# A decoder layer on one core: where sixteen small products for the denominators are issued within a projection

## The chip, the cores and the metric

One core of one Trainium2 chip runs the whole kernel as one program. The metric is the device time of one execution in microseconds. Engines are TensorE (PE; its weight loads are listed apart as PEld), VectorE (DVE), ScalarE (ACT), GpSimd (POOL) and SyncE (SP, here the queue that issues most DMAs).

## What is computed

A post-norm decoder layer on x and a context, both (16, 512, 512), f32. Cut to the part around the change:

```python
qkv = x @ Wqkv.T                                   # 16 heads of 32
q, k = elu(q) + 1, elu(k) + 1
running_kv   = decay_scan(k * v)                   # out[t] = decay * out[t-1] + in[t]
running_ksum = decay_scan(k)
den = clip(sum(q * running_ksum, over a head's 32 channels), 1e-6)
out = q * running_kv / den
g = sigmoid(out @ Wgate.T + bgate)
out = (g * out + (1 - g) * v) @ Wout.T
x = layernorm(x + out)
x = layernorm(x + x * scan_0.9(ctx * ctx))
x = layernorm(x + ffn(x))                          # 4-bit weights, 16-bit activations, SiLU gate
```

## The kernel before

There are three phases: weights are split and quantised, then the attention phase, then the feed-forward phase. The attention phase takes the 16 batch entries one after the other in a pipeline of steps. Step s has a *front* half for batch entry s (q, k and v projections, scans, denominators, the quotient) and a *back* half for entry s - 1 (gate, output projection, the two layer norms). Step 0 has only a front, step 16 only a back, and steps 1 to 15 have both. Each engine has its program written out by hand in its own block, and semaphores join them; an engine executes its list in order.

Full products are made at about f32 precision from three fp32r matmuls of a high and a low half each (`product`, L761: high x high at L767, high x low at L768, low x high at L771), four times over the 512 contraction rows (k = 0 to 3). So one tile of a projection is twelve matmuls of 512 columns. `product` takes a function `between`, which it calls in each of the four rounds k, after the second matmul and ahead of the third.

The *denominators* are 16 products in each step: for each of four row groups j and each of four channel groups c, `qks[:, c]` (q times the running sum of keys, 128 x 128) is the stationary side and `head_sum[:, c]` (128 x 16, which adds up the channels of a head) the moving one, in plain f32 (L820). They land in `den_bank`, a part of the PSUM bank `qk_ps0`. The first call, j = 0, waits for `qks_ready`, that VectorE's last product L553 of the step has been written; the last matmul of j = 3 raises `den_ready`. In the trace each of these products is two instructions of 16 columns, 32 in a step; below they are called the narrow matmuls.

TensorE's order in a step with both halves is: q, k, v of the first channel tile (`qkv(s, 0)`), the gate's four tiles, `qkv(s, 1)`, the context carry, `qkv(s, 2)`, `qkv(s, 3)`, then the output projection in four tiles (`project`), whose results go alternately to two banks `mix_ps`. Between rounds of its second tile stand the denominators; inside its fourth, at k = 1, stands the turn of their reciprocals (L828), and behind it the broadcast of these over the channels (L836).

Who waits for what around that: VectorE adds each projection tile to the residual (`first_residual`, L590). Its order there is L553 `qks`, the residual of tile 0, the last scan and product of the front, two splits of the next x (L534), three local sums (L598), the residual of tile 1, then `reciprocals` (L631 to L637), which waits for `den_ready`. TensorE's turn (L828) waits for `recl_ready`, the last of these. Tiles 2 and 3 of the projection wait for the residual of the tile two before them. In step 0, which has no projection, the 16 products are issued one behind the other.

Of the kernel before, what the change touches and what calls it, by code (L numbers as in the profile page):

```python
# [20 lines left out]
TT = T // P  # L21
# [208 lines left out]
def attention_phase(nc, xT, x, ctx_in, b_gate, decay_in, wah, wal, x2_dram, amax_x2):  # L230
# [3 lines left out]
    with ExitStack() as ctx:  # L234
# [89 lines left out]
        with nc.Block() as block:  # L324
# [432 lines left out]
            def _(pe):  # L757
# [3 lines left out]
                def product(out, stat, mov, between=None):  # L761


                    n = len(stat)
                    for k in range(n):
                        (sh, sl_), (mh, ml) = stat[k], mov[k]
                        pe.matmul(out, sh, mh, start=(k == 0), stop=False)  # L767
                        pe.matmul(out, sh, ml, start=False, stop=False)  # L768
                        if between:
                            between(k)  # L770
                        mm = pe.matmul(out, sl_, mh, start=False, stop=(k == n - 1))  # L771
                    return mm
# [8 lines left out]
                def qkv(b, c):  # L781
                    n = KC * b + c
                    if c == 0:
                        pe.wait_ge(xl_ready, KC * (b + 1))


                    wait(pe, phi_ready, n - 1)
                    product(qk_ps[c % 2][:, 0], w_tile(0, c), x_halves)
                    product(qk_ps[c % 2][:, 1], w_tile(1, c), x_halves).then_inc(qk_ready, 1)
                    wait(pe, v_copied, n - 1)  # L790
                    if c == 0:
                        wait(pe, o_ready, KC * b)
                    product(v_ps[c % 2][:], w_tile(2, c), x_halves).then_inc(v_ready, 1)

                def gate(s):
                    pe.wait_ge(ol_ready, KC * s)
                    for m in range(KC):
                        if m >= 2:
                            pe.wait_ge(gated, KC * (s - 1) + m - 1)
                        product(mix_ps[(m + 1) % 2][:], w_tile(3, m), a_halves).then_inc(gate_ready, 1)  # L800

                def project(s, tiles, between=None):
                    if 0 in tiles:
                        pe.wait_ge(ml_ready, KC * s)
                    for j in tiles:
                        if j == 0:
                            pe.wait_ge(gated, KC * (s - 1) + 3)
                        elif j == 1:
                            pe.wait_ge(scanned, TT * s)
                        else:  # L810
                            pe.wait_ge(y_ready[0], TT * (s - 1) + j - 1)
                        stat = [tuple(h[:, k].rearrange("p (q j) -> p j q", j=TT)[:, j] for h in (ah, al)) for k in range(KC)]
                        mov = [(wah[:, k, 4], wal[:, k, 4]) for k in range(KC)]
                        product(mix_ps[(j + 1) % 2][:], stat, mov, between).then_inc(proj_ready, 1)

                def denominators(s, j):
                    if j == 0:
                        pe.wait_ge(qks_ready, KC * (s + 1))
                    for c in range(KC):
                        mm = pe.matmul(den_bank[:, j], qks[:, c, j * P:(j + 1) * P], head_sum[:, c],  # L820
                                       start=(c == 0), stop=(c == KC - 1))
                    if j == TT - 1:
                        mm.then_inc(den_ready, 1)

                def turn_reciprocals(s):
                    pe.wait_ge(recl_ready, s + 1)
                    for j in range(TT):
                        mm = pe.matmul(turn_bank[:, j * P:(j + 1) * P], rec_halves[:, j], ident_r[:], start=True, stop=True)  # L828
                    mm.then_inc(turned_ready, 1)

                def broadcast(s):

                    pe.wait_ge(rec_turned_ready, s + 1)
                    pe.wait_ge(v_copied, KC * (s + 1))
                    for c in range(KC):
                        pe.matmul(bc_banks[c], head_bc[:, c], rec_turned[:], start=True, stop=True).then_inc(bc_ready, 1)  # L836

                def context_carry(s):
                    pe.wait_ge(sql_ready, s)
                    pe.wait_ge(gated, KC * s)  # L840
                    product(carry_bank, [(strip_h[:], strip_l[:])], [(csq_h[:], csq_l[:])]).then_inc(carry_ready, 1)

                def step(s, front, back):
                    if front:
                        qkv(s, 0)
                    if back:
                        gate(s)
                    if front:
                        qkv(s, 1)
                    if back:  # L850
                        context_carry(s)
                    if front:
                        qkv(s, 2)
                        qkv(s, 3)
                    if back:
                        project(s, (0,))
                    if front and back:
                        project(s, (1,), lambda j: denominators(s, j))
                        project(s, (2,))
                        project(s, (3,), lambda k: turn_reciprocals(s) if k == 1 else None)  # L860
                    elif back:
                        project(s, (1, 2, 3))
                    else:
                        for j in range(TT):
                            denominators(s, j)
                        turn_reciprocals(s)
                    if front:
                        broadcast(s)

                step(0, True, False)  # L870
                with pe.Fori(0, (NB - 2) // 2) as i:
                    for u in range(2):
                        step(2 * i + 1 + u, True, True)
                step(NB - 1, True, True)
                step(NB, False, True)

# [998 lines left out]
```

## Time and profile before

| | us |
|---|---|
| median of 3 runs | 2744.77 (2744.38 to 2745.86) |
| the profiled execution | 2746.06 |
| its span, first to last instruction | 2744.3 |
| TensorE matmuls busy in the span | 2592.1 (94%) |
| TensorE weight loads | 2173.3 (79%) |
| VectorE | 1986.0 (72%) |
| ScalarE | 1362.9 (50%) |
| GpSimd | 404.6 (15%) |
| attention phase in the span | about 60 to 1090 |
| mean granted clock of TensorE | 0.973 |

The profile is of one execution, taken by the hardware profiler. Matmuls are pipelined: a matmul is listed with some 0.39 us, but the next one starts 0.23 us behind it, so the distance between starts is what one costs. The granted clock is given as a share: 1.00 is the upper level of TensorE's clock (2.4 GHz), 0.50 the lower (1.2 GHz). A view of stretches has these columns: the stretch, its length, busy time (and instructions started) of PE, PEld, DVE, ACT and POOL, then the granted clock, the DMA engines' busy share and GB/s. A row of a timeline gives start, length, engine, line, operation and tiles, the count of merged instructions, and in brackets the idle time before with what ended it.

### The profile page before, as it was taken

What the parts mean: (1) busy time and instruction counts of PE and PEld (TensorE: products, weight loads), DVE (VectorE), ACT (ScalarE), POOL (GpSimd) and SP (SyncE); (2) the same over time, 40 slices, a digit from 0 to 9 for tenths busy, and PEclk for the clock granted to TensorE, in tenths of its full rate; (3) what the DMA queues carried; (4) which work ended last, traced back from release to release, by engine and by line L of the source; (5) the groups of instructions that cost most, each with busy time, mean ns of one, the idle gap of its engine ahead of it and who ended that gap; (6) DMA issues with size and microseconds to landing.
All of it is one profiled execution on the core that took longest, in us unless ns stands there. A gap on an engine that the chain in (4) does not pass through costs nothing.

```text
span 2744.3 us, 32949 instructions
## 1 busy us (share of the span) xinstructions
PE 2592.1 (94%) x11584; PEld 2173.3 (79%) x11584; DVE 1986.0 (72%) x2689; ACT 1362.9 (50%) x1716; POOL 404.6 (15%) x277
## 2 busy tenths in 40 slices
PE   2999999999999995799999999999999889999998
PEld 1788888888888884588888887888888668888886
DVE  6688888888888885355555556987777776666664
ACT  2355555555555544333333336988888712222222
POOL 2000000000000000000000002322222143333332
PEclk7899999999999997899999999999999989999999
DMA  5102111111122111655555447776677554455552
GB/s 206 47 26 98 61 61 69 61 61 61 67 90 80 61 54 46 207 193 188 188 188 183 168 155 268 282 271 252 254 260 258 213 223 199 199 208 206 217 220 104
DMA packets 146960, 429.24 MB, mean 156 GB/s; under 512 B 74848, under 2 KB 83296, under 8 KB 106592
## 3 DMA queue, kind: packets, MB, share of 16 engines
q1 hardware_dynamic: 144176, 408.72, 40.9%
q10 hardware_dynamic: 2736, 19.92, 1.8%
q8 instruction: 25, 0.41, 0.1%
q14 instruction: 23, 0.19, 0.0%
HBM read 234.62 MB, written 177.21 MB: 150 GB/s over the span
## 4 chain that ended last, share of the span: by engine, by line
PE 55%; DMA 2%; issue 1%; DVE 1%; ACT 1%; POOL 0%; SPq 0%; POOLq 0%; DVEq 0%; ACTq 0%
PE ff_ps L1759 12%; PE ff_ps L1761 12%; PE ff_ps L1760 12%; PE ff_ps L1811 6%; PE ff_ps L1813 6%; PE ff_ps L1812 6%; DMA ff_raw<-x_rows 0%; PE ff_ps L1769 0%; DMA ff_gs<-gate_ints 0%; DMA ff_q<-x_ints 0%; DMA ff_raw<-gate_products 0%; DMA up_products<-ff_group 0%; ACT ff_up_abs L1285 0%; DVE ff_lo L1703 0%; DMA gate_products<-ff_group 0%
## 5 line engine op out<-in xcount | busy, mean ns | idle before, releaser
L1759 PE MATMUL ff_ps<-ff_hi,ff_wh 128*128 128x512 f32 x1536 | 601.4, 392 | 43.7 <-DVE ff_lo L1473 40.3
L1760 PE MATMUL ff_ps<-ff_lo,ff_wh 128*128 128x512 f32 x1536 | 599.7, 390 | 0.0
L1761 PE MATMUL ff_ps<-ff_hi,ff_wl 128*128 128x512 f32 x1536 | 599.6, 390 | 0.0
L1296 ACT ACTIVATE ff_group<-ff_ps,ff_scales 128x512 f32<-128x512 f32 x384 | 258.2, 687 | 317.2 <-PE ff_ps L1761 305.8
L1759 PEld LDWEIGHTS ff_ps<-ff_hi,ff_wh 128*128 128x128 f32 x1536 | 289.7, 189 | 104.3 <-DVE ff_lo L1473 40.6
L1761 PEld LDWEIGHTS ff_ps<-ff_hi,ff_wl 128*128 128x128 f32 x1536 | 289.7, 189 | 60.4
L1760 PEld LDWEIGHTS ff_ps<-ff_lo,ff_wh 128*128 128x128 f32 x1536 | 289.9, 189 | 59.9
L1811 PE MATMUL ff_ps<-ff_wh,ff_hi 128*128 128x512 f32 x768 | 299.6, 390 | 25.1 <-DVE ff_lo L1697 23.7
L1812 PE MATMUL ff_ps<-ff_wl,ff_hi 128*128 128x512 f32 x768 | 299.2, 390 | 0.0
L1813 PE MATMUL ff_ps<-ff_wh,ff_lo 128*128 128x512 f32 x768 | 299.2, 390 | 0.0
L1487 DVE TENSOR_REDUCE ff_gate_max<-ff_group 128x2048 f32 (+1 forms) x48 | 109.7, 2286 | 208.3 <-ACT ff_group L1296 208.3
L1447 ACT ACTIVATE ff_hi<-ff_sr 128x2048 fp32r<-128x2048 int16 x47 | 90.2, 1920 | 337.8 <-PE ff_ps L1813 325.9
L767 PE MATMUL qk_ps<-xh,wah 128*128 128x512 f32 x512 | 202.7, 396 | 18.8 <-DVE xl L534 18.8
L1703 DVE TENSOR_TENSOR ff_lo<-ff_sr,ff_hi 128x2048 fp32r<-128x2048 int16 x47 | 109.3, 2326 | 139.6 <-ACT ff_hi L1447 139.6
L768 PE MATMUL qk_ps<-xl,wah 128*128 128x512 f32 x512 | 200.8, 392 | 0.0
L771 PE MATMUL qk_ps<-xh,wal 128*128 128x512 f32 x512 | 200.4, 391 | 0.0
L391 POOL TENSOR_TENSOR rstd<-var_eps,mhalf 128x4 f32<-128x4 f32 x32 | 49.7, 1554 | 982.0 <-DVE var_eps L579 982.0
L1811 PEld LDWEIGHTS ff_ps<-ff_wh,ff_hi 128*128 128x128 f32 x768 | 144.5, 188 | 55.8 <-issue 24.1
L442 ACT ACTIVATE squares_out<-xrow,neg_mean 128x512 f32<-128x512 f32 x128 | 91.6, 717 | 165.2 <-DVE neg_mean L574 165.2
L1812 PEld LDWEIGHTS ff_ps<-ff_wl,ff_hi 128*128 128x128 f32 x768 | 144.5, 188 | 30.1
L1813 PEld LDWEIGHTS ff_ps<-ff_wh,ff_lo 128*128 128x128 f32 x768 | 144.4, 188 | 30.0
L1511 DVE CUSTOM_DVE_ANT_0 ff_up_abs<-ff_gs,ff_up_abs 128x512 f32<-128x512 int16 x192 | 158.4, 880 | 0.0
(204 smaller groups left out, 5039.1 us busy)
## 6 DMA issues: line engine op xcount, KB each, us to landing
gate_products<-ff_group SPq DMA_DIRECT2D x48, 1024.0 KB, 4.0
ff_raw<-gate_products SPq DMA_DIRECT2D x48, 1024.0 KB, 5.6
up_products<-ff_group SPq DMA_DIRECT2D x48, 1024.0 KB, 4.3
ff_raw<-up_products SPq DMA_DIRECT2D x48, 1024.0 KB, 9.2
gate_ints<-ff_gs SPq DMA_DIRECT2D x48, 512.0 KB, 2.6
ff_gs<-gate_ints SPq DMA_DIRECT2D x48, 512.0 KB, 9.9
xt_raw<-in_xT SPq DMA_DIRECT2D x64, 256.0 KB, 2.8
csq<-in_ctx_rows SPq DMA_DIRECT2D x16, 1024.0 KB, 6.8
```

The costliest lines, as they stand in the source:

```text
L767: pe.matmul(out, sh, mh, start=(k == 0), stop=False)
L768: pe.matmul(out, sh, ml, start=False, stop=False)
L771: mm = pe.matmul(out, sl_, mh, start=False, stop=(k == n - 1))
L1296: act.activation(group[:, g, m * T:(m + 1) * T], out_ps[(GM * g + m) % 6][:], ACT.Copy, scale=s_x).then_inc(evacuated, 1)
L1487: dve.tensor_reduce(gate_max[:, 0, bass.ds(t, 1)], group[:, g], AX.X, ALU.max).then_inc(gate_max_ready, 1)
L1511: dve.tensor_tensor_reduce(up_abs[:, sl, cols], gs16[:, g, cols], up_abs[:, sl, cols], 1.0, -3e38, ALU.mult, ALU.max, cells[:, sl, m:m + 1 ...
L1759: pe.matmul(o, wh[:, m, k], hi[:, par, k], start=(k == 0), stop=False)
L1760: pe.matmul(o, wh[:, m, k], lo[:, par, k], start=False, stop=False)
L1761: mm = pe.matmul(o, wl[:, m, k], hi[:, par, k], start=False, stop=(k == KC - 1))
L1811: pe.matmul(o, hi[:, sl, k, rows], mh, start=(g == 0 and k == 0), stop=False)
L1812: pe.matmul(o, hi[:, sl, k, rows], ml, start=False, stop=False)
L1813: mm = pe.matmul(o, lo[:, sl, k, rows], mh, start=False, stop=(g == NG - 1 and k == KC - 1))
```

## The change

In steps with both halves the sixteen products were called four at a time, `denominators(s, j)` in round j of the second projection tile. Now all four calls are made in round k = 1, j = 0 to 3 one after the other, and rounds 0, 2 and 3 have none. Their order among each other, the wait of the first and the semaphore of the last are as they were. Step 0 and step 16 are not touched.

```diff
--- before.py
+++ after.py
@@ -855,7 +855,7 @@
                     if back:
                         project(s, (0,))
                     if front and back:
-                        project(s, (1,), lambda j: denominators(s, j))
+                        project(s, (1,), lambda k: [denominators(s, j) for j in range(TT)] if k == 1 else None)
                         project(s, (2,))
                         project(s, (3,), lambda k: turn_reciprocals(s) if k == 1 else None)
                     elif back:
```

## Rows read from the trace of the kernel before

**Rows 1.** Page, parts 1 and 2: TensorE's busy time, and its granted clock in 40 slices.
```profile
PE 2592.1 (94%) x11584; PEld 2173.3 (79%) x11584; DVE 1986.0 (72%) x2689; ACT 1362.9 (50%) x1716; POOL 404.6 (15%) x277
PEclk7899999999999997899999999999999989999999
```

**Rows 2.** Busy time of each engine in the attention part's steady stretch.
```profile
175.00:1037.00 862.00, 862.00 (x3970) 739.05 (x3969) 749.72 (x1314) 477.17 (x768) 45.31 (x28) 1.00 0.17 67
```

**Rows 3.** Waits of that stretch: us in total, times, longest us.
```profile
PEld qk_ps L820 <- DVE qks L553: 3.1, 14, 0.2
```

**Rows 4.** Timeline, TensorE's matmuls: start, us, engine, line, out<-in, count.
```profile
531.50 0.40 PE L767 MATMUL mix_ps<-wah,ah 128*128 128x512 f32 x1
...
532.04 1.06 PE L820 MATMUL qk_ps<-head_sum,qks 128*128 128x16 f32 x8
...
533.39 0.41 PE L767 MATMUL mix_ps<-wah,ah 128*128 128x512 f32 x1
...
533.86 0.96 PE L820 MATMUL qk_ps<-head_sum,qks 128*128 128x16 f32 x8
534.67 0.60 PE L771 MATMUL mix_ps<-wah,al 128*128 128x512 f32 x1
535.11 0.40 PE L767 MATMUL mix_ps<-wah,ah 128*128 128x512 f32 x1
...
538.54 0.40 PE L767 MATMUL mix_ps<-wah,ah 128*128 128x512 f32 x1
...
539.25 0.39 PE L767 MATMUL mix_ps<-wah,ah 128*128 128x512 f32 x1
```

**Rows 5.** Timeline, TensorE's weight loads inside the second group of narrow matmuls.
```profile
533.86 0.41 PEld L820 LDWEIGHTS qk_ps<-head_sum,qks 128*128 128x128 f32 x3
...
534.64 0.31 PEld L771 LDWEIGHTS mix_ps<-wah,al 128*128 128x128 f32 x1
```

**Rows 6.** Timeline, VectorE around the second tile, and L828's weight loads.
```profile
531.30 0.68 DVE L553 TENSOR_TENSOR qks<-phi,qks 128x512 f32<-128x512 f32 x1
...
538.81 0.69 DVE L590 SCALAR_TENSOR_TENSOR xrow<-mix_ps,xrow 128x512 f32<-128x512 f32 x1 [0.91 <-PE mix_ps L771]
...
540.68 0.22 DVE L637 TENSOR_TENSOR rec_halves<-den_rec,rec_halves 128x64 fp32r<-128x64 f32 x1
...
542.31 0.46 PEld L828 LDWEIGHTS qk_ps<-ident_r,rec_halves 128*32 128x32 f32 x4
```

**Rows 7.** Step 0's run: timeline, then stretches with busy times and clock.
```profile
102.97 6.48 PE L820 MATMUL qk_ps<-head_sum,qks 128*128 128x16 f32 x32 [3.19 <-DVE qks L553]
...
103.00:103.50 0.50, 0.50 (x5) 0.50 (x5) 0.50 (x1) 0.00 (x0) 0.00 (x0) 1.00 0.00 0
103.70:109.60 5.90, 5.75 (x27) 5.64 (x27) 4.27 (x8) 1.53 (x3) 0.00 (x0) 0.50 0.49 132
114.00:117.20 3.20, 3.20 (x8) 2.38 (x8) 3.20 (x6) 2.21 (x4) 0.00 (x0) 0.50 0.68 268
```

**Rows 8.** After step 15: timeline of TensorE, then stretches with busy times and clock.
```profile
1036.01 0.40 PE L771 MATMUL mix_ps<-wah,al 128*128 128x512 f32 x1
...
1036.90 0.62 PE L836 MATMUL v_ps<-rec_turned,head_bc 32*128 32x512 f32 x2
...
1064.30 0.63 PE L768 MATMUL mix_ps<-wal,ah 128*128 128x512 f32 x1
...
1068.99 0.63 PE L767 MATMUL mix_ps<-wah,ah 128*128 128x512 f32 x1
...
1038.00:1039.00 1.00, 0.00 (x0) 0.00 (x0) 1.00 (x2) 1.00 (x4) 0.00 (x0) 0.92 0.00 0
1042.00:1045.60 3.60, 3.33 (x8) 2.65 (x9) 3.60 (x9) 2.94 (x4) 0.00 (x0) 0.50 0.02 5
1063.00:1069.50 6.50, 5.82 (x14) 4.62 (x15) 3.31 (x7) 0.00 (x0) 0.00 (x0) 0.50 0.50 161
```

## Prediction

> **What bounds the kernel now.** I read the page first. TensorE is busy for 94% of the span and its granted clock is at 9 tenths or more almost everywhere [rows 1]. The change touches the attention part alone, so next I took the busy time by stretches. From 175 to 1037 us TensorE is busy in every microsecond (862.00 of 862.00) at a granted clock of 1.00, with VectorE at 87% of the stretch and ScalarE at 55% [rows 2]. In the view of waits of that stretch no row has TensorE's matmuls waiting for anybody. The one wait that concerns this change is of the weight load ahead of the denominators, on VectorE's product `qks`: 3.1 us in 14 times, 0.2 us each [rows 3]. So in the fifteen steps that have both halves (s = 1 to 15) the time is the sum of what TensorE issues, one matmul after the other, and everything that shortens or stretches this chain shows in full. The reader should see in [rows 4] how that chain looks inside the second projection tile: two full matmuls, eight narrow ones (16 moving columns; each of the four products of a call is two instructions, so a step has 32), one full matmul, four times over.
>
> **The change, part by part.** No instruction is removed or added; 24 of the 32 narrow matmuls of a step move within one tile, and the one wait on `qks_ready` moves from round 0 to round 1. No DMA is in it, and no queue but TensorE's is touched.
>
> *What a round costs.* A round without narrow matmuls is 539.25 - 538.54 = 0.71 us, or 0.235 for each full matmul. A round with eight is 535.11 - 533.39 = 1.72. That splits so: from L767 to the first narrow matmul 0.47 (two ordinary distances, so going in costs nothing); from there to L771 0.81; from L771 to the next L767 0.44 where 0.235 is ordinary, so coming out costs 0.21 extra at that place [rows 4]. How far apart the narrow ones are I take from the weight loads, which set the pace: the second load starts at 533.86 and that of L771, seven loads later, at 534.64, which is 0.111 us each [rows 5].
>
> *One run in place of four.* 24 further pairs at 0.111 make 2.67, so from the first narrow matmul to L771 it is 0.81 + 2.67 = 3.48, and the round is 0.47 + 3.48 + 0.44 = 4.39. The tile becomes 4.39 + 3 x 0.71 = 6.52 us. Before, it would be 4 x 1.72 = 6.88 without the wait: 0.36 us saved in a step.
>
> *The wait.* Round 0 took 533.39 - 531.50 = 1.89, which is 0.17 over its sisters, because `qks` ended at 531.30 + 0.68 = 531.98, after the first narrow matmul could have gone [rows 4, 6]. In the changed kernel the run begins one plain round later, at about 531.50 + 0.71 + 0.47 - 0.23 = 532.45 for its first weight load, so half a microsecond after `qks`. The wait is then met already; queued behind it are the whole run and the rest of the tile, and nobody waits longer. A wait that is already met costs nothing: the load of L828 behind its own met wait starts at 542.31, as early as it can [rows 6]. Saved: 0.17.
>
> *Who is late next.* The tile ends 0.53 us sooner. VectorE's first residual for this tile sat idle 0.91 us for TensorE, so it follows down. The clipping and reciprocals stand behind that residual in VectorE's order, so denominators that are ready sooner start nothing sooner; their last part ends at 540.68 + 0.22 = 540.90, and TensorE asks for it at 542.31, of which 0.53 goes: 0.9 us are left [rows 6]. So I expect no new wait. Without anything else the change is worth 15 x (0.36 + 0.17) = 8.0 us less.
>
> *The clock.* That is where I expect it to go the other way. The trace has one run of all 32 narrow matmuls already: step 0 has no projection and issues them alone, in 6.48 us, or 0.20 each. It starts at clock 1.00 (five matmuls in the half microsecond from 103.00), the clock drops to 0.50, its lower level of 1.2 GHz, and it stays there through 5.9 us of narrow matmuls that follow each other without a gap, to the end of the run [rows 7]. So such a run does not bring the clock back. At the end of step 15 the clock drops within 1038 to 1039, little more than 1 us behind the last matmuls, which were 32 rows high; the last full ones start at 1036.0, so under 3 us without full matmuls were enough there [rows 8]. In the kernel before, by contrast, the narrow matmuls come in pieces of 0.8 us with full ones between, and the clock stays at 1.00 in all steps [rows 2, 4]. The changed kernel has 3.48 us in one piece, in each of 15 steps. No row shows such a piece following a busy stretch, but the two nearest ([rows 7, 8]) both have the clock low, so I take it that the clock falls during or right behind the run, in nearly every step, and then full matmuls run at the lower level until it is given back.
>
> *What one fall costs.* Full matmuls at the lower level are (1068.99 - 1064.30) / 11 = 0.426 us apart in place of 0.235, so of a low stretch 45% is lost. The three low stretches of full matmuls in the attention part are 3.20, 3.33 and 5.82 us busy, hence 1.4, 1.5 and 2.6 us lost, 1.8 in the mean [rows 7, 8]. Narrow ones of the run that are still to come after a fall add 0.20 - 0.11 = 0.09 us each; how many that is no row shows, so I leave it in the upper end. As a bound below: a fall costs nothing at all if it does not come. I take 1.8 for each of 15 steps: 15 x (1.8 - 0.53) = 19 us more. The ends are 15 x (1.4 - 0.53) = 13 and 15 x (2.6 - 0.53) = 31.
>
> The Trainium skill (TensorE: Matmul & The Clock Gate, "Why this matters for your kernels") says that the clock is kept by leaving no idle gaps between matmul bursts, and wins its upper level by keeping TensorE continuously busy. By that rule the run, which has no gap, would leave the clock up, and the whole change would come out at the 8.0 us less of the first rival below. The rows of step 0's run speak against reading it so: busy without a gap, and the clock stayed down.
>
> **The rivals.**
> First, *the clock holds*. The narrow matmuls with their full 128-column weight loads may count for enough, and the run is 3.5 us, not the 6.5 of step 0, where TensorE also had been idle just before. Then the saving stands: 2746.1 - 8.0 on the profiled execution, 2737 on the runs' median, faster by 0.29%. It decides where the array's activity in the run is enough to hold a clock that is up, though it isn't enough to raise one that is down; the trace doesn't separate the two. Against it stands [rows 8], where a shorter stretch did.
> Second, *it falls in some steps only*, since each step would meet whatever the chip looks at in another phase. With 3 to 7 falls it is 3 x 1.8 - 8.0 = -2.6 to 7 x 1.8 - 8.0 = +4.6 us, which is no change (2742 to 2749, middle 2746).
> Third, *the narrow matmuls are slow in a long run for another reason*, 0.20 each from the supply of instructions and not from the clock: 32 x 0.20 = 6.4 in place of 3.5 us, 15 x (2.9 - 0.5) = 36 more, 2781. Against it: the first five of step 0's run took 0.5 us at clock 1.00 [rows 7].
>
> **How the numbers follow.** The profiled execution took 2746.1 us (span 2744.3), 1.3 over the median of the runs, 2744.8. The forecast is 2746.1 + 19.4 - 1.3 = 2764 us. Chances: the clock falls in most steps (8 or more) 0.70; it holds 0.17; it falls in some 0.10; a long run is slow by itself 0.03. Of this kernel about 0.2%, 5.5 us, can be told from no change. Slower by more: 0.70 + 0.03 and less a hundredth or two for few falls, 0.72; within: 0.11; faster: 0.17. The range reaches from the lower part of the second rival, 2741, to the upper end of the forecast, 31 more plus a microsecond for narrow matmuls at the lower level, 2777. It leaves out the first rival and the third, 2 in 10. The forecast's own range is 2751 (eight falls) to 2777.
>
> **What would show it.** The second projection tile with one piece of 32 narrow matmuls, no wait on `qks`, and where the clock is up a length of 6.5 us: then the first two terms are right. In the stretch that now has clock 1.00, the clock's mean should come down to some 0.95, with a low stretch behind or inside each run and full matmuls 0.43 us apart there; from step to step the distance should grow by about 1.3 us. If the clock reads 1.00 throughout, the first rival holds; if the run takes 0.2 us for each matmul at clock 1.00, the third. The prediction is wrong if a narrow matmul counts for more than I take from step 0, or if a fall costs much less than 1.8 us. If TensorE shows a new wait on VectorE between the tiles, my account of who is late next has failed.

## The result and the profile after

The changed kernel takes 2768.27 us (median of 6 runs, 2764.68 to 2770.54), the kernel before 2745.32 in the runs beside it: 1.0082 times as long, with a 95% interval of 1.0069 to 1.0095. So it is 23 us slower, on the forecast's side; the forecast was 2764. The profiled execution took 2764.68 us, its span 2763.0.

The page of the changed kernel, busy times and granted clock:

```profile
PE 2611.7 (95%) x11584; PEld 2186.2 (79%) x11584; DVE 1987.2 (72%) x2689; ACT 1360.4 (49%) x1716; POOL 401.4 (15%) x277
PEclk8899999999999998799999999999999989999999
```

TensorE issues the same 11584 matmuls as before and is busy 20 us longer. That is all the page tells, since a tenth is too coarse for the clock. The steady stretch of the attention part tells more (columns as in [rows 2]):

```profile
175.00:1060.00 885.00, 884.54 (x3970) 753.85 (x3969) 750.21 (x1318) 477.05 (x769) 45.30 (x28) 0.96 0.17 65
```

It holds the 3970 matmuls that took 862 us in [rows 2], and the mean clock is 0.96 where it was 1.00. TensorE is as full as before (884.54 of 885 us), so nobody makes it wait; its instructions take longer. The length of the steps is best read from the broadcast L836, which stands once at each step's end. The source view of that line, first and last start, in the kernel before and in the changed one:

```profile
L836 PE MATMUL qk_ps<-rec_turned,head_bc x32: 388/492/791, 112.2 to 1036.7; 32*128 32x512 f32 x32
```

```profile
L836 PE MATMUL qk_ps<-rec_turned,head_bc x32: 388/492/787, 112.2 to 1058.7; 32*128 32x512 f32 x32
```

Fifteen steps took 924.5 us and take 946.5: 22.0 more, which is the whole loss but for a microsecond. (In the two profiled executions the totals differ by 18.6 only, because the feed-forward part happened to be 3 us shorter in the second; more on that with the third experiment.)

Now the second projection tile in three steps of the changed kernel, TensorE's timeline. First a step in which the clock holds:

```profile
225.02 0.39 PE L768 MATMUL mix_ps<-wal,ah 128*128 128x512 f32 x1
225.25 3.64 PE L820 MATMUL qk_ps<-head_sum,qks 128*128 128x16 f32 x32
228.74 0.60 PE L771 MATMUL mix_ps<-wah,al 128*128 128x512 f32 x1
229.18 0.40 PE L767 MATMUL mix_ps<-wah,ah 128*128 128x512 f32 x1
```

This is the tile as the prediction laid it out: one piece of 32, no wait ahead of it, 228.74 - 225.25 = 3.49 us to L771 (3.48 was worked out), 0.44 to the next L767. Only steps 1 and 2 look so. Then two in which it falls:

```profile
350.10 3.68 PE L820 MATMUL qk_ps<-head_sum,qks 128*128 128x16 f32 x32
353.62 0.77 PE L771 MATMUL mix_ps<-wah,al 128*128 128x512 f32 x1
354.20 0.63 PE L767 MATMUL mix_ps<-wah,ah 128*128 128x512 f32 x1
354.62 0.63 PE L768 MATMUL mix_ps<-wal,ah 128*128 128x512 f32 x1
...
357.10 0.40 PE L768 MATMUL mix_ps<-wal,ah 128*128 128x512 f32 x1
```

```profile
286.19 4.53 PE L820 MATMUL qk_ps<-head_sum,qks 128*128 128x16 f32 x32
290.56 0.77 PE L771 MATMUL mix_ps<-wah,al 128*128 128x512 f32 x1
...
291.98 0.63 PE L771 MATMUL mix_ps<-wah,al 128*128 128x512 f32 x1
...
295.40 0.47 PE L768 MATMUL mix_ps<-wal,ah 128*128 128x512 f32 x1
295.70 0.40 PE L771 MATMUL mix_ps<-wah,al 128*128 128x512 f32 x1
```

In the step at 350 the run has its full pace to its last matmuls, and then the full ones are 0.43 us apart instead of 0.235 until 357. In the step at 286 the run itself takes 4.37 us to L771, since its last part goes at half pace, and full matmuls are slow until 295.4. The stretches with their clock:

```profile
223.80:230.00 6.20, 6.20 (x44) 6.16 (x44) 6.06 (x12) 0.81 (x2) 0.00 (x0) 1.00 0.16 48
289.00:296.00 7.00, 7.00 (x23) 5.97 (x23) 4.21 (x11) 1.08 (x3) 0.00 (x0) 0.53 0.26 75
354.00:357.00 3.00, 3.00 (x8) 2.35 (x8) 1.30 (x2) 0.00 (x0) 0.00 (x0) 0.50 0.48 167
```

From step 3 on the two kinds take turns. The broadcasts of three steps in a row (a broadcast stands at a step's end, so each distance is one step):

```profile
426.93 0.73 PE L836 MATMUL qk_ps<-rec_turned,head_bc 32*128 32x512 f32 x2
...
489.26 0.72 PE L836 MATMUL qk_ps<-rec_turned,head_bc 32*128 32x512 f32 x2
...
553.19 0.73 PE L836 MATMUL qk_ps<-rec_turned,head_bc 32*128 32x512 f32 x2
```

They are 62.33 and 63.93 us apart. The broadcasts of steps 1 and 2, of which the second has no fall, and two of the kernel before:

```profile
175.80 0.72 PE L836 MATMUL qk_ps<-rec_turned,head_bc 32*128 32x512 f32 x2
...
236.73 0.72 PE L836 MATMUL qk_ps<-rec_turned,head_bc 32*128 32x512 f32 x2
```

```profile
483.23 0.73 PE L836 MATMUL qk_ps<-rec_turned,head_bc 32*128 32x512 f32 x2
...
544.69 0.73 PE L836 MATMUL qk_ps<-rec_turned,head_bc 32*128 32x512 f32 x2
```

A step without a fall takes 60.93 us and one of the kernel before 61.46. So a fall costs 1.4 us or 3.0 us. The broadcasts of all fifteen steps give the count: steps 1 and 2 have none, steps 3, 5 and so on to 15 (seven) take 63.92 to 63.94 us, and steps 4, 6 and so on to 14 (six) take 62.33 to 62.36. That is 13 falls in 15 steps.

### The profile page after: what moved, and what is told of

Same layout as the page of the kernel before. It is cut to its first block, busy times and chain, and to the rows that moved or that the text cites. A ratio compares the mean times of both kernels' runs of the same rounds, so it can differ in the third digit from the quotient of the medians.

```text
span 2763.0 us, 32949 instructions
## 1 busy us (share of the span) xinstructions
PE 2611.7 (95%) x11584; PEld 2186.2 (79%) x11584; DVE 1987.2 (72%) x2689; ACT 1360.4 (49%) x1716; POOL 401.4 (15%) x277
## 4 chain that ended last, share of the span: by engine, by line
PE 55%; DMA 2%; issue 1%; DVE 1%; ACT 1%; POOL 0%; SPq 0%; POOLq 0%; DVEq 0%; ACTq 0%
PE ff_ps L1759 12%; PE ff_ps L1760 12%; PE ff_ps L1761 12%; PE ff_ps L1811 6%; PE ff_ps L1812 6%; PE ff_ps L1813 6%; DMA ff_raw<-x_rows 0%; PE ff_ps L1769 0%; DMA ff_gs<-gate_ints 0%; DMA ff_q<-x_ints 0%; DMA ff_raw<-gate_products 0%; DMA up_products<-ff_group 0%; ACT ff_up_abs L1285 0%; DVE ff_lo L1703 0%; DMA gate_products<-ff_group 0%
## 5 line engine op out<-in xcount | busy, mean ns | idle before, releaser
L767 PE MATMUL qk_ps<-xh,wah 128*128 128x512 f32 x512 | 203.1, 397 | 19.4 <-DVE xl L534 19.4
L771 PE MATMUL qk_ps<-xh,wal 128*128 128x512 f32 x512 | 200.9, 392 | 0.0
```

## The experiments

Two theories stood against each other. *The clock*: a long piece of matmuls with 16 moving columns keeps too little of TensorE's array at work, the clock goes to its lower level, and full matmuls pay for it; the merging itself saves time. *The run*: a long run of these products costs by itself, by its length, whatever the array does.

**1. The same run with a wide moving side.** In steps with a projection the 32 matmuls stream 128 columns (an identity matrix) in place of the 16 of `head_sum`, in one run (`w1_wide_run`) and in the four pieces of before (`w2_wide_pieces`). Both kernels leave the denominators out. The diff has the two calls one below the other, that of the run first.

```diff
-                def denominators(s, j):
+                def denominators(s, j, wide=False):
...
-                        mm = pe.matmul(den_bank[:, j], qks[:, c, j * P:(j + 1) * P], head_sum[:, c],
-                                       start=(c == 0), stop=(c == KC - 1))
+                        out, mov = (qk_ps[0][:, 0, j * P:(j + 1) * P], ident[:]) if wide else (den_bank[:, j], head_sum[:, c])
+                        mm = pe.matmul(out, qks[:, c, j * P:(j + 1) * P], mov, start=(c == 0), stop=(c == KC - 1))
...
-                        project(s, (1,), lambda j: denominators(s, j))
+                        project(s, (1,), lambda k: [denominators(s, j, True) for j in range(TT)] if k == 1 else None)
...
+                        project(s, (1,), lambda j: denominators(s, j, True))
```

> The changed kernel, but in steps with a projection the 32 narrow matmuls stream 128 columns (the identity) in place of 16, into the same PSUM bank; stationary sides, weight loads, count and place of the run are the same. It leaves out the denominators themselves: what lands in the bank is not their sum by heads. Theory (the clock falls because narrow matmuls keep too little of the array at work): a run as long in time but with a full moving side holds the clock, 1.00 in every step, and if the pace stays that of the weight loads (0.11 us each) only the saving is left, 8 us under the kernel before, about 2737; each 0.01 us of slower pace adds 15 x 32 x 0.01 = 4.8 us. Rival (a long run of these products costs by itself, whatever it streams): as the changed kernel, about 2768, with the clock down or not.

> The kernel before with the same 128 columns in its four pieces of eight: the base for the wide run. It leaves out the denominators as the wide run does. If the pace is that of the weight loads, 2745 as before; the difference to the wide run is then the saving alone, 15 x 0.53 = 8 us by the theory. By the rival the wide run is 20 us or so over this one.

Measured: the wide run 2736.64 us, 0.9969 of the kernel before (0.9958 to 0.998); the wide pieces 2745.06, 1.0001 (0.9992 to 1.0011). The wide run's timeline and its steady stretch:

```profile
347.94 3.73 PE L821 MATMUL qk_ps<-ident,qks 128*128 128x128 f32 x32
351.43 0.60 PE L771 MATMUL mix_ps<-wah,al 128*128 128x512 f32 x1
```

```profile
170.00:1030.00 860.00, 860.00 (x3994) 741.21 (x3994) 753.83 (x1327) 479.76 (x774) 45.30 (x28) 1.00 0.18 67
```

The run is again 3.49 us from its first matmul to L771, with as many weight loads in the same place; what differs is how much streams past them. The clock is 1.00 in the whole stretch, each step after the first takes 60.93 us, and the loss has turned into the gain of 8 us that the sum had without a fall. The rival of the run falls with this: it had 2768. Wide pieces cost what narrow ones do (fifteen steps take 924.3 us, 924.5 with narrow ones), which fits a pace that the weight loads set.

**2. Two pieces, apart and near.** 16 narrow matmuls in each of two rounds of the tile: once in rounds 1 and 3 (`e1_two_apart`), once in rounds 1 and 2 (`e2_two_near`). The number of pieces and their length are the same.

```diff
-                        project(s, (1,), lambda j: denominators(s, j))
+                        project(s, (1,), lambda k: [denominators(s, j) for j in (k - 1, k)] if k in (1, 3) else None)
```

```diff
-                        project(s, (1,), lambda j: denominators(s, j))
+                        project(s, (1,), lambda k: [denominators(s, j) for j in (2 * k - 2, 2 * k - 1)] if k in (1, 2) else None)
```

> Two pieces of 16 narrow matmuls, in rounds 1 and 3 of the second projection tile, with full matmuls between. Theory: a piece is 1.7 us and full matmuls stand on both sides, so the clock holds at 1.00; two exits of 0.12 us and the wait of 0.17 are saved in each step, 15 x 0.41 = 6 us under the kernel before, about 2739. Rival (a price that grows with the length of the run): about half of the changed kernel's loss, 2755.

> The same two pieces of 16 in rounds 1 and 2, so only three full matmuls (0.7 us) lie between them. Theory: what counts is how little full work there is around, not the length of one piece, so the clock falls in part of the steps: over the two pieces apart, between 2745 and 2766. If the length of a piece decides, it equals the two pieces apart, 2739.

Measured: apart 2737.86 us, 0.9974 (0.9964 to 0.9985); near 2762.17, 1.0059 (1.0043 to 1.0074). The steady stretch of the one and of the other:

```profile
170.00:1030.00 860.00, 860.00 (x3988) 740.90 (x3987) 752.85 (x1325) 479.88 (x774) 45.26 (x28) 1.00 0.18 67
```

```profile
170.00:1060.00 890.00, 890.00 (x3969) 757.43 (x3969) 751.71 (x1321) 478.17 (x771) 45.29 (x28) 0.96 0.17 65
```

And a tile of the near one:

```profile
353.28 1.85 PE L820 MATMUL qk_ps<-head_sum,qks 128*128 128x16 f32 x16
354.99 0.60 PE L771 MATMUL mix_ps<-wah,al 128*128 128x512 f32 x1
355.43 0.40 PE L767 MATMUL mix_ps<-wah,ah 128*128 128x512 f32 x1
355.66 0.39 PE L768 MATMUL mix_ps<-wal,ah 128*128 128x512 f32 x1
355.89 2.76 PE L820 MATMUL qk_ps<-head_sum,qks 128*128 128x16 f32 x16
358.49 0.77 PE L771 MATMUL mix_ps<-wah,al 128*128 128x512 f32 x1
```

The first piece takes 354.99 - 353.28 = 1.71 us to L771 and the second 2.60: in this step the clock falls inside it, though neither piece has more matmuls than in the variant apart, whose clock holds. Three full matmuls between the pieces were not enough to keep it; six were. So the length of one piece isn't what decides; how much full work stands between the pieces does. "Part of the steps" in the expectation was too weak: the profiled execution has a fall in all fifteen. (It is the longest of four, 2771.97 us, 10 over their median.) Its fifteen steps take 952.9 us and those of the variant apart 918.7, so a fall costs 34.2 / 15 = 2.3 us here too. The variant apart beats the kernel before and the changed one.

**3. Half of the products: the saving by itself.** With two of four channel groups (half of the denominators' sums is left out) a step has 16 narrow matmuls, and merging them brought no fall: all steps after the first take the same time to 0.02 us. In four pieces of 4 (`h1_half_pieces`), one run in round 1 (`h2_half_run`), one run in round 0 (`h3_half_run_k0`).

```diff
-                    for c in range(KC):
+                    for c in range(2):
...
-                                       start=(c == 0), stop=(c == KC - 1))
+                                       start=(c == 0), stop=(c == 1))
```

> The kernel before with half of the denominators' products (two of four channel groups, so the sums lack the other half): four pieces of 4 narrow matmuls. It is the base for the next two. Each narrow matmul at 0.11 us: 15 x 16 x 0.11 = 26.7 us less in the steps 1 to 15, and about 16 x 0.20 = 3.2 less in step 0, so 2715. If a piece has a price of its own, that stays in it.

> The same half of the products in one run of 16 in round 1. The run is 1.7 us and full matmuls are on both sides, so by the theory the clock holds at 1.00 and what shows is the saving alone: three exits of 0.12 us and the wait of 0.17, 15 x 0.53 = 8 us under the four pieces of 4. Rival (joining pieces costs by itself): over them. If the exits cost nothing and only the wait went, 2.6 us under.

> The same run of 16 in round 0, where the wait on VectorE's last product still stands ahead of it. Theory: 15 x 0.17 = 2.6 us over the run in round 1, and one wait of 0.2 us on it in each step. If a met wait costs as much as one that is not, no difference.

Measured: 2718.40, 2707.18 and 2712.33 us. The first is 3 us over its expectation: the fifteen steps give 26.2 of the 26.7 us, but the first broadcast comes only 1.6 us sooner (110.6 against 112.2) where 3.2 was expected of step 0. That makes 2 us of the 3; the rest lies outside. Source view of L836 in this order:

```profile
L836 PE MATMUL qk_ps<-rec_turned,head_bc x32: 392/492/787, 110.6 to 1008.9; 32*128 32x512 f32 x32
```

```profile
L836 PE MATMUL qk_ps<-rec_turned,head_bc x32: 388/492/792, 110.6 to 1000.9; 32*128 32x512 f32 x32
```

```profile
L836 PE MATMUL qk_ps<-rec_turned,head_bc x32: 388/494/787, 111.0 to 1003.9; 32*128 32x512 f32 x32
```

Fifteen steps take 898.3, 890.3 and 892.9 us. So merging saves 8.0 us, and of that the wait on `qks` is 2.6 and the three exits 5.4: 0.53, 0.17 and 0.36 in a step, as in the prediction's sum. The totals differ by more, 11.2 and 5.1. For the first of these the traces show where 2 to 3 us come from: the feed-forward part of the pieces has a stretch of low clock behind a short pause of TensorE, and that of the run has none there.

```profile
1656.00:1662.00 6.00, 4.56 (x11) 3.60 (x12) 6.00 (x5) 6.00 (x7) 0.00 (x0) 0.53 0.80 284
```

```profile
1645.00:1655.00 10.00, 7.21 (x32) 5.98 (x33) 9.36 (x11) 9.97 (x11) 2.24 (x2) 1.00 0.78 298
```

TensorE pauses for 2.8 us in the second too (7.21 busy of 10), but its clock stays up. The same place in the kernel before and in the changed one:

```profile
1684.00:1690.00 6.00, 5.02 (x12) 3.96 (x13) 6.00 (x6) 6.00 (x7) 0.05 (x1) 0.50 0.74 262
```

```profile
1704.00:1712.00 8.00, 5.19 (x23) 4.31 (x24) 7.34 (x7) 8.00 (x10) 0.21 (x1) 1.00 0.79 295
```

There the clock is down before and up after: at 0.43 us in place of 0.235 the 5.02 us of matmuls lose 2.3 us, most of the 3 us by which the totals differ less than the steps. What makes it fall or not at this place I didn't test. Between the runs in round 1 and in round 0 the remaining 2.5 us lie outside the fifteen steps as well; I leave them open.

**4. Three quarters of the products.** One run of 24 matmuls in round 1 (`h4_three_quarters_run`; the changed kernel with three channel groups, the last at `c == 2`).

> Three of four channel groups (the sums lack one), one run of 24 narrow matmuls in round 1, 2.6 us. With the clock at 1.00 throughout it would be 15 x 8 x 0.11 = 13.3 us and 1.6 us of step 0 over the run of 16. Theory: the clock falls in part of the steps, fewer than for 32, and each fall adds 1.4 to 2.6 us; between 15 and 50 us over the run of 16, low stretches in the trace. If there is a sharp length between 24 and 32, none falls and it is 15 us over.

Measured: 2740.80 us, 0.9985 of the kernel before (0.9977 to 0.9994). One of its twelve executions took 5315.78 us, which nothing here explains; without it the median is 2740.52. Its steps and a tile:

```profile
L836 PE MATMUL qk_ps<-rec_turned,head_bc x32: 388/492/787, 110.6 to 1033.9; 32*128 32x512 f32 x32
```

```profile
345.57 2.75 PE L820 MATMUL qk_ps<-head_sum,qks 128*128 128x16 f32 x24
348.17 0.79 PE L771 MATMUL mix_ps<-wah,al 128*128 128x512 f32 x1
348.75 0.63 PE L767 MATMUL mix_ps<-wah,ah 128*128 128x512 f32 x1
...
351.31 0.54 PE L767 MATMUL mix_ps<-wah,ah 128*128 128x512 f32 x1
```

The steps take 923.3 us: 33.0 over the run of 16, of which 13.3 are the 120 further matmuls at 0.111 and 19.7 the clock. It falls in 14 of 15 steps, right behind the run or in its last few matmuls (the run grows from 2.60 us to 2.76 over the steps), for 1.4 us each. The expectation had fewer falls than with 32, and there was one more. So a run of 24, 2.6 us long, loses the clock nearly as often as one of 32, and one of 16 keeps it; between 16 and 24 nothing was tried. With a quarter of the products left out this kernel is only 4 us faster than the one before.

**5. A version that keeps the run and the clock.** The first experiment says what to do: fill the moving side up. The matrix of head sums gets zero columns, 128 in place of 16 (`v1_wide_heads`) or 64 (`v2_heads_64`), and the denominators stand in the first 16 of each group of columns in the bank. The whole computation is done.

```diff
-        head_sum = sb("head_sum", [P, KC, NH])
+        head_sum = sb("head_sum", [P, KC, P])
...
-        den_bank = qk_ps[0][:, 0, 0:TT * NH].rearrange("p (j h) -> p j h", h=NH)
+        den_all = qk_ps[0][:, 0].rearrange("p (j h) -> p j h", h=P)
+        den_bank = den_all[:, :, 0:NH]
...
-                        mm = pe.matmul(den_bank[:, j], qks[:, c, j * P:(j + 1) * P], head_sum[:, c],
+                        mm = pe.matmul(den_all[:, j], qks[:, c, j * P:(j + 1) * P], head_sum[:, c],
```

> The changed kernel with the head sums' matrix padded by zero columns from 16 to 128, so that the run of 32 streams 128 columns and the true denominators stand in the first 16 of each group. The whole computation is done. Theory: as the wide run, the clock holds in every step, 60.93 us from step to step, 2737. If it is what stands in the columns that counts and not their number, zeros would let the clock fall as 16 columns do, 2768.

> The same with 64 columns, half of the wide run's. The whole computation is done. If the work of the array decides, this lies between: no less than 2737 (clock holds) and no more than 2768 (falls in nearly all steps); I take the upper half as likelier, since half-filled stretches are near where the clock fell in step 15's end. The pace of the products should stay 0.11 us, as both 16 and 128 columns have it.

> The two pieces of 16 in rounds 1 and 3 once more, on the same chip as the padded versions, to rank them: 61.05 us from step to step against 60.93, so 1.8 us over the padded run of 32 if that holds the clock.

Measured: with 128 columns 2734.13 us, 0.9958 of the kernel before (0.9944 to 0.9972); with 64, 2737.98, 0.9972 (0.9961 to 0.9983); the two pieces apart again 2739.35, 0.998 (0.9971 to 0.9989). With 128 columns, the steady stretch and the run of step 0:

```profile
170.00:1028.00 858.00, 858.00 (x3986) 739.13 (x3985) 752.33 (x1322) 479.57 (x772) 45.35 (x28) 1.00 0.18 67
```

```profile
103.52 5.42 PE L821 MATMUL qk_ps<-head_sum,qks 128*128 128x128 f32 x32 [3.19 <-DVE qks L554]
```

The same of the version with 64:

```profile
170.00:1028.00 858.00, 858.00 (x3984) 739.67 (x3984) 753.53 (x1324) 478.59 (x771) 45.28 (x28) 1.00 0.18 68
```

```profile
103.45 6.82 PE L821 MATMUL qk_ps<-head_sum,qks 128*128 128x64 f32 x32 [3.19 <-DVE qks L554]
```

Both hold the clock in steps 1 to 15, and every step from 2 on takes 60.93 us. I had thought 64 columns likelier to lose it, and that was wrong. Columns of zeros did as well here as the identity of the first experiment, itself mostly zeros. The difference between the two comes up to the broadcast of step 1 (3.5 us in the profiled executions). It begins in step 0, whose run takes 5.42 us with 128 columns and 6.82 with 64. The end of that run, with 128 columns and with 64:

```profile
107.00:109.00 2.00, 1.94 (x18) 1.74 (x16) 1.52 (x3) 0.38 (x1) 0.00 (x0) 1.00 1.02 290
```

```profile
107.00:110.00 3.00, 3.00 (x16) 3.00 (x15) 1.44 (x3) 1.18 (x3) 0.00 (x0) 0.50 0.89 296
```

With 128 columns the clock is back at 1.00 within the run, and with 64 it is not. That is one profiled execution of each. The padded version with 128 columns has the lowest median of all kernels here that do the whole computation, 11 us under the kernel before. Its interval overlaps those of the other two, so its lead over them is likely and not shown.

## Why the prediction was right, point by point

- *What bounds the kernel.* TensorE's chain in the attention part, and everything in it shows in full: right. No wait of TensorE appeared with the change, and the steps grew by what its own matmuls grew.
- *The saving.* 0.36 us for the exits and 0.17 for the wait in each step were worked out from single rows. A step without a fall is 60.93 us against 61.46, so 0.53; the third experiment gives 5.4 and 2.6 us for fifteen steps, 8.0 together. Right in each part.
- *The clock falls, in most steps.* The forecast had this at 0.70 from two places of the trace in which less than full work had gone ahead. It falls in 13 of 15 steps of the profiled execution. That it is the clock, and that it hangs on the moving side, is shown by the wide run and by the padded versions: same count, same weight loads, same place, same 3.49 us, and no fall. Whether it is the columns that go in or those that are written out can't be told apart, since both grow together.
- *The price of a fall.* This term was undersized: 1.8 us forecast, and (22.0 + 15 x 0.53) / 13 = 2.3 measured. Two kinds of step, 1.4 and 3.0 us, take turns. The forecast's mean came from full matmuls alone ([rows 7, 8]); in the dear kind the last part of the run is at half pace as well (4.37 us in place of 3.49), which the prediction named and kept in its upper end only. That is 0.8 to 0.9 of the 3.0 us, so the full matmuls behind the run lose 2.1 in the dear kind and 1.4 in the cheap one, (7 x 2.1 + 6 x 1.4) / 13 = 1.8 in the mean. So the 1.8 holds for the full matmuls, and what the sum left out is the run's own slow end, 0.5 a fall. That the 1.8 fits so well has luck in it: it was the mean of three stretches that stand behind pauses of TensorE, and no row tied their length to this place. On the other side the forecast counted 15 falls and there were 13, which took back 3.6 of the 6.5 us that the price was short. (19 and 19.4 in its text are one sum, rounded twice.) Together: 27 forecast and 30 measured for the falls in fifteen steps, which is most of the 4 us between 2764 and 2768. (The profiled execution is the shortest of the six, 2764.68 us: there the shorter feed-forward part took these 3 us back.)
- *The rivals.* That the clock holds, as it would by the Trainium skill (TensorE: Matmul & The Clock Gate, "Why this matters for your kernels") if leaving no idle gaps between matmul bursts were all that is needed: refuted here, since TensorE was busy for 884.54 us of the 885 from 175 on, and all 13 falls lie in these. What its time would have been, 2737, is what the wide run has (2736.64). That a long run is slow by itself: refuted by the same run and by the pace of 0.11 us in the steps where the clock holds. That it falls in a few steps only: no profiled execution showed that; the clock fell in 13, 14 or all 15 steps, or in none.
- *The signs named ahead.* One piece of 32, no wait on `qks`, 6.5 us for the tile where the clock is up: seen. Mean clock 0.95: 0.96. Growth of 1.3 us from step to step: 22.0 / 15 = 1.5.

## What to carry to other kernels

Matmuls with few moving columns are busy time for the profile, and yet the clock can fall on them: 32 in one run with 16 columns each left it at 0.50 in 13 of 15 steps, and the full matmuls behind paid, while in four pieces, or with 64 or 128 columns, the clock stayed at 1.00. So look, before merging small products into one run to save a pipeline's exits, at how the granted clock behaved where the trace already has such a run, and either leave full matmuls between the pieces or pad the moving side where columns cost no time (here 0.11 us a matmul with 16, 64 and 128 alike). And price both signs of an edit: here 8 us of true saving stood against 30 us of a consequence, and the page's busy share showed neither.

## What the runs showed of the hardware that was not expected

- In plain f32, 32 matmuls on fresh 128 x 128 weights take 3.49 us to the next full matmul with 16, 64 and 128 moving columns alike; up to there more columns took no more time.
- With the moving side padded to 64 columns the clock stayed at 1.00 through all runs of 3.49 us, but in step 0, where it was at 0.50, it did not come back within the run (6.82 us), and with 128 it did (5.42 us). So what kept the clock up did not raise it there.
- The falls settle into a pattern. With the run of 24 each costs 1.4 us and fifteen steps take 923.3 us, nearly the 924.5 of the whole kernel before, though they have 120 matmuls less; with the run of 32 cheap and dear steps take turns. Why they settle so is open: no run here was made to show it. That the steps with 24 and those of the kernel before come out alike, 61.45 us, is not explained either.
